# A transformer layer on one NeuronCore: layer-norm sums kept in PSUM, the f32r split handed to ScalarE and GpSimd, and another order of all engines

## The chip, the cores and the metric

One NeuronCore of a Trainium2 chip runs the whole program. The metric is the device time in microseconds (us) of one execution; lower is better. Before the change it is 1008.31 us, the median of three runs (1006.66 to 1008.78).

## What is computed

A batch of 32 sequences of 256 tokens with 128 features passes through one layer: softmax attention with 8 heads (no output projection; each head's values are 128 wide and the heads are summed), a layer norm without scale and shift, a gated feed-forward part with two more hidden layers, and a second layer norm. The reference, cut:

```python
Q = (x @ Wq.T).reshape(b, n, 8, 64)
K = (x @ Wk.T).reshape(b, n, 8, 64)
V = (x @ Wv.T).reshape(b, n, 8, 128)
attn = softmax(einsum('bnhr,bmhr->bhnm', Q, K), axis=-1)
x1 = layernorm(x + einsum('bhnm,bmhd->bnd', attn, V))
h = silu(tlin(x1, w1, s1)) * tlin(x1, w2, s2)      # 128 -> 512
h = gelu(tlin(h, h1, sh1)); h = gelu(tlin(h, h2, sh2))   # 512 -> 512, exact gelu
out = layernorm(x1 + tlin(h, w3, s3))              # tlin(x, w, s) = (x @ w.T) * s
```

Everything is float32.

## The kernel before

**Arithmetic.** TensorE multiplies in float32r. To keep float32 accuracy every operand is split in a high part (a copy rounded to float32r) and a low part (the difference), and a product is three matmuls: high by high, high by low, low by high. The feed-forward weights are ternary, so their low parts are zero; a flag made at run time (`lo_flag`) chooses at a branch on TensorE (line 2009) between a body with and one without these matmuls. The run takes the body without them, and there a feed-forward product is two matmuls.

**Tiles and stages.** The work goes in 16 pairs of sequences (512 tokens, index `i` or `k`). For each pair TensorE makes queries and keys (`query_or_key`, 8 of them, `t` = 0..7), values (`values`, 8), scores (`scores`, 8 groups of 12 matmuls that use 64 rows of the array each and run two at a time), then for each of the 16 head and sequence combinations `u` it turns the normalised probabilities (`turn_prob`, 4 transposes) and multiplies them with the values (`times_v`, 6 matmuls) into PSUM bank 7. The sum over heads is copied to `at` and turned (`turn_attention`), the residual is added (`res_add`), normalised (`stats1_of`, `rstd1_of`, `norm1`) to `x1`, turned again (`turn_x1`), and goes through `layer1_z1`, `layer1_z2`, `layer2`, `layer3`, `layer4` and `turn_y`; `y_add`, `stats2_of`, `rstd2_of` and `norm2` make the output. The last pair's feed-forward part is done in two halves (`..._half`).

**Who does what.** ScalarE (ACT) makes the exponentials, tanh and gelu, and rounds PSUM results to high parts (`t_high`, `v_high`, `pt_high`). VectorE (DVE) makes maxima, reciprocals (`inverse`), low parts of PSUM results (`t_low`, `v_low`, `pt_low`), the gate, and the layer norms. GpSimd (POOL) scales the probabilities in place (`norm`), makes `rstd` by a power, and shares with ACT and DVE the rounding and differences of the hidden activations (`high` and `low`), which lie in SBUF.

**Order.** There is no scheduler at run time. Each engine's order is written out by hand: a start, a loop body `for k in range(1, LAST)` that is unrolled 14 times (on TensorE the function `cycle`), and an end (`last`). In a cycle attention of pair `k`, the queries of pair `k + 1` and the feed-forward part of pair `k - 1` (its third layer's second half and fourth layer: of pair `k - 2`) are interleaved. Engines wait for each other by semaphores; the tuples such as `(s_silu, k - 1, KC, 1)` behind a TensorE step name what it waits for, mostly so that a PSUM bank (the tables `T_BANK` to `YT_BANK`) is free.

**What the steps of the prediction touch.** `norm1` (line 982) reads `res`, mean and rstd from SBUF and writes `x1`; `turn_x1` waits for both halves of it. `res_add` (958) writes its sum to `res` in SBUF, `y_add` (1027) to `y` in SBUF. SyncE (SP) issues all transfers in one queue. The second pair's input is issued last of those at the start:

```python
sp.dma_start(w3_in...); sp.dma_start(res[:, :, :], x_rows[0])...
load_xt(1)      # waits until the single buffer xt_in has been split
```

On ACT `xt_high(1)`, which needs it, stands between `t_high(0, 3)` and `t_high(0, 4)`.

Of the kernel before, what the change touches and what calls it, by code (L numbers as in the profile page):

```python
# [9 lines left out]
ALU = mybir.AluOpType  # L10
# [20 lines left out]
L3_BANK = (2, 5, 0, 6)
L4_BANK = (2,)
YT_BANK = (3,)
# [5 lines left out]
def need(eng, sem, value):  # L39
# [6 lines left out]
T_OTHER = {(0, 0): 1, (0, 1): 5, (0, 2): 2, (0, 4): 3, (0, 5): 1, (0, 6): 1, (0, 7): 5, (1, 0): 4, (1, 1): 5,  # L46
    (1, 2): 4, (1, 4): 2, (1, 5): 3, (1, 7): 5}
V_OTHER = {(0, 0): 2, (0, 2): 3, (0, 3): 1, (0, 5): 1, (0, 6): 0, (0, 7): 2, (1, 0): 0, (1, 1): 2, (1, 2): 0,
    (1, 3): 1, (15, 4): 6, (15, 6): 4, (15, 7): 1}
SC_OTHER = {(0, 0): (5, 6), (0, 1): (3, 0), (0, 2): (1, 6), (0, 3): (4, 0), (0, 4): (3, 2), (0, 5): (5, 3),  # L50
    (0, 6): (1, 6), (0, 7): (5, 1), (1, 0): (6, 4), (1, 1): (5, 3), (1, 2): (4, 6), (15, 3): (2, 6),
    (15, 4): (1, 3), (15, 5): (0, 1), (15, 6): (4, 3), (15, 7): (5, 6)}
TURN_OTHER = {(0, 1): 5, (0, 2): 6, (0, 3): 1, (0, 4): 6, (0, 6): 5, (0, 7): 2, (0, 8): 3, (0, 9): 5, (0, 10): 0,
    (0, 11): 1, (0, 12): 5, (0, 13): 2, (0, 14): 3, (0, 15): 4, (15, 2): 5, (15, 3): 4, (15, 4): 5, (15, 5): 2,
    (15, 6): 3, (15, 7): 4, (15, 8): 6, (15, 9): 2, (15, 11): 1, (15, 12): 4, (15, 13): 5, (15, 14): 2}
AT_OTHER = {(0, 0): 0, (14, 1): 3, (15, 0): 3, (15, 1): 5}
X1T_OTHER = {(14, 0): 4}
Z1_OTHER = {(14, 2): 0, (14, 3): 1}
Z2_OTHER = {(14, 0): 3, (14, 1): 1, (14, 2): 2}
L2_OTHER = {(14, 0): 1, (14, 1): 0, (14, 2): 5, (14, 3): 2}  # L60
L3_OTHER = {(14, 0): 5, (14, 1): 0, (14, 2): 2}
L4_OTHER = {(13, 0): 0, (14, 0): 4}
YT_OTHER = {(13, 0): 0, (14, 0): 5}


X1T_HALF = (5, 3)
Z1_HALF = ((4, 3, 4, 5), (5, 0, 3, 2))
Z2_HALF = ((7, 2, 0, 4), (4, 4, 5, 2))
L2_HALF = ((1, 2, 7, 6), (4, 1, 3, 7))
L3_HALF = ((0, 5, 6, 2), (4, 3, 0, 7))  # L70
L4_HALF = (1, 6)
YT_HALF = (5, 4)


def layer_kernel(nc, x, x_t, wq_t, wk_t, wv_t, w1_t, w2_t, h1_t, h2_t, w3_t, scales_t, out):
# [14 lines left out]
    def there(i):  # L90
        return 0 <= i < PAIRS
# [5 lines left out]
    with ExitStack() as ctx:  # L97
# [38 lines left out]
        with ExitStack() as early:  # L136
# [11 lines left out]
        x1 = sb("x1", [P, TT, D])  # L148
# [101 lines left out]

        def slot(i, u, ring):
            return (i * J + u) % ring
# [13 lines left out]
        def _(sp):  # L266
            sp.dma_start(xt_in[:, :], x_t[0]).then_inc(s_xin, 16)
            sp.dma_start(wq_in[:, A], wq_t[:, A]).then_inc(loads["wqa"], 16)
            sp.dma_start(wk_in[:, A], wk_t[:, A]).then_inc(loads["wka"], 16)
            sp.dma_start(wq_in[:, B_], wq_t[:, B_]).then_inc(loads["wqb"], 16)  # L270
            sp.dma_start(wk_in[:, B_], wk_t[:, B_]).then_inc(loads["wkb"], 16)
            sp.dma_start(wv_in[:, :], wv_t).then_inc(loads["wv"], 16)
            sp.dma_start(scales[:, :], scales_t).then_inc(s_scales, 16)
            sp.dma_start(w1_in[:, :], w1_t).then_inc(loads["w1"], 16)
            sp.dma_start(w2_in[:, :], w2_t).then_inc(loads["w2"], 16)
            sp.dma_start(h1_in[:, :, :], h1_t.rearrange("(c p) o -> p c o", p=P)).then_inc(loads["h1"], 16)
            sp.dma_start(h2_in[:, :, :], h2_t.rearrange("(c p) o -> p c o", p=P)).then_inc(loads["h2"], 16)
# [38 lines left out]
        def _(pool):  # L316
# [1738 lines left out]
```

## Time and profile before

| | |
|---|---|
| median of three runs | 1008.31 us |
| the profiled execution | 1008.28 us |
| its span (first to last instruction) | 1006.5 us |
| mean granted TensorE clock | 0.988 of full |
| busy: PE, DVE, ACT, POOL | 966.8, 882.9, 797.4, 502.2 us |
| length of one cycle, turn_prob(k, 0) to turn_prob(k + 1, 0), k = 2 to 14 | 60.7 us |

PE is TensorE's matmul side and PEld its weight loads, DVE is VectorE, ACT ScalarE, POOL GpSimd and SPq SyncE's queue. L982 is line 982 of the kernel. Times of rows are microseconds from the start of the span unless marked ns. A granted clock of 1.00 is 2.4 GHz, 0.50 is 1.2 GHz.

### The profile page before, as it was taken

To read this page: it belongs to the slowest core of one execution; us is meant where nothing else is said; L and a number is where in the kernel's file an instruction comes from. 1 tells how busy PE (TensorE), PEld (TensorE's weight loads), DVE (VectorE), ACT (ScalarE), POOL (GpSimd) and SP (SyncE) were. 2 spreads that over 40 slices of the span, in tenths; PEclk is the share of its full clock that TensorE was granted. 3 is DMA by queue.
4 is the path that set the end of the run, shared out by engine and by line. 5 is a ranking of instruction groups with operands and counts; after the bars stand their busy time and mean duration, and the time that the engine had idled before them with its cause. 6 is when DMAs were issued, how large, how long until landed. Compare 5 with 4: busy or idle time off the path is not lost.

```text
span 1006.5 us, 19738 instructions
## 1 busy us (share of the span) xinstructions
PE 966.8 (96%) x6553; PEld 821.3 (82%) x6553; DVE 882.9 (88%) x1846; ACT 797.4 (79%) x1958; POOL 502.2 (50%) x520
## 2 busy tenths in 40 slices
PE   4979999999999999999999999999999999999997
PEld 3868888888888888888888888888888888888886
DVE  4988798898988989898898988989898898988886
ACT  3958878888888878878788888878878788888844
POOL 3954354553546345444453545445454553546644
PEclk8989999999999999999999999999999999999999
DMA  5000000000000000010000000000010000000000
GB/s 188 12 13 11 2 21 1 22 11 22 12 2 22 11 22 11 2 32 2 22 12 14 21 1 23 11 22 11 1 33 1 22 12 1 22 1 11 12 11 22
DMA packets 22055, 17.83 MB, mean 18 GB/s; under 512 B 1088, under 2 KB 18496, under 8 KB 21952
## 3 DMA queue, kind: packets, MB, share of 16 engines
q1 hardware_dynamic: 21952, 16.53, 5.6%
q8 instruction: 56, 0.92, 0.4%
q14 instruction: 47, 0.39, 0.1%
HBM read 12.33 MB, written 4.19 MB: 16 GB/s over the span
## 4 chain that ended last, share of the span: by engine, by line
PE 86%; DVE 8%; issue 2%; POOL 1%; DMA 1%; SPq 1%; ACT 1%; POOLq 0%; DVEq 0%; ACTq 0%
PE bank L1567 13%; PE bank L1568 12%; PE bank L1455 12%; PE bank L1449 11%; PE bank L1451 11%; PE bank L1450 10%; PE bank L1498 10%; DVE x L982 5%; PE bank L1547 3%; PE bank L1548 3%; DVE y L1027 1%; DMA xt_in<-in_x_t 1%; DVE res L958 1%; DVE stats L964 1%; PE bank L1627 1%
## 5 line engine op out<-in xcount | busy, mean ns | idle before, releaser
L327 POOL TENSOR_TENSOR prob<-prob,inv_total 128x512 f32<-128x512 f32 x256 | 272.3, 1072 | 179.2 <-DVE inv_total L943 179.2
L538 ACT ACTIVATE prob<-bank,neg_max 128x256 f32<-128x256 f32 x512 | 238.0, 480 | 8.3 <-DVE neg_max L937 7.7
L260 DVE TENSOR_TENSOR pt_lo<-bank,pt_hi 128x512 fp32r<-128x512 f32 x256 | 173.6, 679 | 56.1 <-ACT pt_hi L263 55.9
L263 ACT ACTIVATE pt_hi<-bank 128x512 fp32r<-128x512 f32 x256 | 152.7, 599 | 43.5 <-PE bank L1455 41.4
L937 DVE TENSOR_REDUCE neg_max<-bank 128x2 f32<-128x512 f32 x256 | 171.9, 678 | 5.6 <-PE bank L1498 5.1
L1455 PE MATMUL bank<-ident,prob 128*128 128x128 f32 x1024 | 155.8, 275 | 5.2 <-POOL prob L327 5.2
L1449 PE MATMUL bank<-pt_hi,v_hi 128*128 128x256 f32 x512 | 158.2, 309 | 0.0
L1455 PEld LDWEIGHTS bank<-ident,prob 128*128 128x128 f32 x1024 | 123.3, 142 | 30.1 <-POOL prob L327 5.4
L1451 PE MATMUL bank<-pt_hi,v_lo 128*128 128x256 f32 x512 | 144.9, 283 | 0.0
L1450 PE MATMUL bank<-pt_lo,v_hi 128*128 128x256 f32 x512 | 144.7, 283 | 0.0
L538 ACT ACTIVATION_READ_ACCUMULATOR prob<-bank,neg_max 128x1 f32 x512 | 109.1, 213 | 0.0
L260 POOL TENSOR_TENSOR odd_lo<-gated,odd_hi 128x512 fp32r<-128x512 f32 (+1 forms) x50 | 62.2, 1244 | 83.5 <-ACT odd_hi L263 82.9
L1449 PEld LDWEIGHTS bank<-pt_hi,v_hi 128*128 128x128 f32 x512 | 97.6, 191 | 5.2 <-issue 0.2
L1450 PEld LDWEIGHTS bank<-pt_lo,v_hi 128*128 128x128 f32 x512 | 97.8, 191 | 3.0
L1567 PE MATMUL bank<-even_hi,h_hi 128*128 128x512 f32 x240 | 98.8, 412 | 0.0
L263 ACT ACTIVATE v_hi<-bank 128x512 fp32r<-128x512 f32 x128 | 76.8, 600 | 26.0 <-PE bank L1451 24.8
L1451 PEld LDWEIGHTS bank<-pt_hi,v_lo 128*128 128x128 f32 x512 | 97.3, 190 | 0.0
L1567 PE MATMUL bank<-odd_hi,h_hi 128*128 128x512 f32 x240 | 97.3, 405 | 0.0
L260 DVE TENSOR_TENSOR v_lo<-bank,v_hi 128x512 fp32r<-128x512 f32 x128 | 87.2, 681 | 10.0 <-ACT v_hi L263 10.0
L263 ACT ACTIVATE t_hi<-bank 128x512 fp32r<-128x512 f32 x128 | 76.3, 598 | 23.7 <-PE bank L1451 19.5
L1568 PE MATMUL bank<-odd_lo,h_hi 128*128 128x512 f32 x240 | 94.8, 395 | 0.0
L260 DVE TENSOR_TENSOR t_lo<-bank,t_hi 128x512 fp32r<-128x512 f32 x128 | 86.3, 676 | 9.7 <-ACT t_hi L263 9.4
(137 smaller groups left out, 2395.7 us busy)
## 6 DMA issues: line engine op xcount, KB each, us to landing
xt_in<-in_x_t SPq DMA_DIRECT2D x16, 256.0 KB, 2.7
res<-in_x SPq DMA_DIRECT2D x16, 256.0 KB, 2.8
out_x<-y SPq DMA_DIRECT2D x15, 256.0 KB, 2.6
h_in<-in_h_t SPq DMA_DIRECT2D x2, 1024.0 KB, 9.1
w_in<-in_w_t SPq DMA_DIRECT2D x3, 256.0 KB, 5.7
wv_in<-in_wv_t SPq DMA_DIRECT2D x1, 512.0 KB, 5.1
out_x<-y SPq DMA_DIRECT2D x2, 128.0 KB, 2.0
wq_in<-in_wq_t SPq DMA_DIRECT2D x1, 192.0 KB, 3.5
```

Of the source, the lines that this page charges most:

```text
L260: return eng.tensor_tensor(dst, src, hi.bitcast(F32), ALU.subtract)
L263: return nc.scalar.activation(dst, src, ACT.Copy)
L327: nc.gpsimd.tensor_tensor(prob[:, s, :, :], prob[:, s, :, :], inv_total[:, u, :].unsqueeze(2).to_broadcast([P, NT, N]), ALU.mult).then_inc ...
L538: last = nc.scalar.activation(prob[:, slot(i, u, RING), nt, :], sc_bank(i, u)[:, nt * N:(nt + 1) * N], ACT.Exp, bias=neg_max[:, u, nt:nt + 1],
L937: nc.vector.tensor_reduce(neg_max[:, u, :], sc_bank(i, u).rearrange("p (t m) -> p t m", m=N), AX.X, ALU.max, negate=True).then_inc(s_max, 1)
L1449: mm(dst, w_hi, m_hi, start=start, stop=False)
L1450: mm(dst, w_hi, m_lo, start=False, stop=False)
L1451: return mm(dst, w_lo, m_hi, start=False, stop=stop)
L1455: last = turn(dst[:, n * P:(n + 1) * P], b, ident[:, :])
L1498: ends.append(mm(sc_bank(i, 2 * g + n)[:, nt * N:(nt + 1) * N], left[rows, t, q], right[rows, t + 1, m], start=(term == 0), stop=(term == 2)))
L1567: mm(dst, w_hi[:, c, cols], m_hi[:, c, :], start=begins, stop=False)
L1568: last = mm(dst, w_hi[:, c, cols], m_lo[:, c, :], start=False, stop=ends and not with_lo)
```

## The change

- **Sums in PSUM.** `res_add` and `y_add` write their sums back into the PSUM bank that they read; `stats1_of`, `norm1`, `stats2_of` and `norm2` read them there. `x1` becomes two buffers that alternate. `load_res` now waits for `res_add` and not for `norm1`; `norm2` takes over the wait for the stored `y`.
- **Casts and differences.** All `high` of the hidden activations (12 for each pair) are on ACT and all `low` (12) on POOL; DVE has neither any more outside the last half steps. Before, a cycle's body had 5 `high` on ACT and 7 on DVE, 7 `low` on POOL and 5 on DVE. `xt_high` moves from POOL to ACT and `xt_low` from DVE to POOL. `norm2(13)` and `norm2(14)` move from POOL to DVE. At the start ACT takes the casts of `wqa`, `wqb`, `wkb` and `wv0`.
- **Another order** on all engines, with new bank tables. In a cycle `scores(k, 3)` and `scores(k, 4)` stand together, and `scores(k, 7)` and `scores(k + 1, 0)`; before only `scores(k + 1, 1)` and `(k + 1, 2)` did. `turn_attention(k - 1, 1)` comes third in the cycle, and `turn_x1(k - 1)` some 10 us behind it. The four `gelu3` of a pair are in two groups now, with exponentials between.
- **Start.** `load_xt(1)` stands behind the load of `wv`. Ten matmuls of `ident` by itself (`WARM`) come first on TensorE, into bank 7. Nearly the whole of pair 0's attention stands before the branch.
- `dynamic_dma_scratch_size` goes from 4096 to 2048.

```diff
+WARM = 10
-        x1 = sb("x1", [P, TT, D])
+        x1 = [sb(f"x1_{n}", [P, TT, D]) for n in range(2)]
+        def tiles_in(psum):
+            return psum.rearrange("p (t d) -> p t d", d=D)
+        def sum1_of(i, b):
+            return tiles_in(at_bank(AT_BANK, AT_OTHER, i, b)[:, 0:N])
+        def sum2_of(f):
+            return tiles_in(at_bank(YT_BANK, YT_OTHER, f, 0)[:, :])
...
             sp.dma_start(wv_in[:, :], wv_t).then_inc(loads["wv"], 16)
+            load_xt(1)
             sp.dma_start(scales[:, :], scales_t).then_inc(s_scales, 16)
...
-                    half = res[:, NT * b:NT * (b + 1), :]
-                    nc.vector.tensor_tensor(half, at_bank(...)[:, 0:N].rearrange(...), half,
+                    turned = sum1_of(i, b)
+                    nc.vector.tensor_tensor(turned, turned, res[:, NT * b:NT * (b + 1), :],
                                             ALU.add).then_inc(s_radd, 1)
...
+            def norm(dst, src, tiles, mv, rstd):
+                for t in tiles:
+                    last = nc.vector.tensor_scalar(dst[:, t, :], src[:, t - tiles[0], :], mv[:, t, 0:1], rstd[:, t:t + 1],
+                                                   ALU.subtract, ALU.mult)
+                return last
...
             def norm1(f, b):
                 if there(f):
-                    dve.wait_ge(s_rs1, after(f, 2, b + 1))
-                    need(dve, s_yadd, f)
-                    for t in range(NT * b, NT * (b + 1)):
-                        last = nc.vector.tensor_scalar(x1[:, t, :], res[:, t, :], mv1[:, t, 0:1],
-                                                       rstd1[:, t:t + 1], ALU.subtract, ALU.mult)
-                    last.then_inc(s_x1, 1)
+                    need(dve, s_yadd, f - 1)
+                    hold(dve, s_rs1, after(f, 2, b + 1))
+                    norm(x1_of(f), sum1_of(f, b), tiles_of(b), mv1, rstd1).then_inc(s_x1, 1)
...
+            pe.wait_ge(s_ident, 1)
+            for _ in range(WARM):
+                mm(acc[:, 0:P], ident[:, :], ident[:, :], start=True, stop=True)
             query_or_key(0, 0)
```

The new cycle on TensorE, from its start to `scores(k, 5)` (the branches for k = 1 left out):

```diff
+turn_prob(k, 0, (s_exp, k, J, 4))
+layer3(k - 2, 0, 1, w)
+turn_attention(k - 1, 1, (s_t_lo, k, H, 7))
+layer3(k - 2, 1, 0, w, (s_exp, k, J, 6))
+turn_prob(k, 1, (s_exp, k, J, 5))
+layer3(k - 2, 1, 1, w)
+turn_prob(k, 2, (s_t_lo, k, H, 8))
+scores(k, 3, (s_x1, k - 1, 2, 1), (s_gelu3, k - 2, KC, 1))
+scores(k, 4, (s_gelu3, k - 2, KC, 2), (s_pt_lo, k, J, 1))
+times_v(k, 0)
+layer3(k - 2, 2, 0, w, (s_pt_lo, k, J, 2))
+values(k, 2, (s_x1, k - 1, 2, 2))
+times_v(k, 1)
+layer3(k - 2, 3, 0, w, (s_pt_lo, k, J, 3))
+values(k, 3, (s_exp, k, J, 7))
+values(k, 4, (s_exp, k, J, 8))
+turn_x1(k - 1, (s_v_lo, k, VT, 3))
+turn_prob(k, 3, (s_exp, k, J, 9))
+layer3(k - 2, 2, 1, w)
+layer3(k - 2, 3, 1, w)
+values(k, 5, (s_v_lo, k, VT, 4))
+turn_prob(k, 4, (s_v_lo, k, VT, 5))
+times_v(k, 2)
+turn_prob(k, 5, (s_pt_lo, k, J, 4))
+layer1_z1(k - 1, 0, w, (s_gelu3, k - 2, KC, 3))
+times_v(k, 3)
+layer1_z1(k - 1, 1, w, (s_x1t_lo, k - 1, 1, 1))
+turn_prob(k, 6, (s_pt_lo, k, J, 5))
+times_v(k, 4)
+query_or_key(k + 1, 0, (s_v_lo, k, VT, 6))
+layer1_z2(k - 1, 0, w, (s_pt_lo, k, J, 6))
+scores(k, 5, (s_gelu3, k - 2, KC, 4), (s_silu, k - 1, KC, 1))
```

ACT's order up to the tanh that this last step waits for:

```diff
+pt_high(k, 0)
+gelu3(k - 2, 0)
+pt_high(k, 1)
+gelu3(k - 2, 1)
+pt_high(k, 2)
+high(k - 2, 3, 0)
+high(k - 2, 3, 1)
+exp(k, 6)
...
+x1t_high(k - 1)
+pt_high(k, 3)
+gelu3(k - 2, 2)
+v_high(k, 5)
+pt_high(k, 4)
+high(k - 2, 3, 2)
+gelu3(k - 2, 3)
+pt_high(k, 5)
+tanh(k - 1, 0)
```

## Rows read from the trace of the kernel before

**Rows 1.** The page: engine PE in all, and granted clock in 40 slices.
```profile
PE 966.8 (96%) x6553; PEld 821.3 (82%) x6553; DVE 882.9 (88%) x1846; ACT 797.4 (79%) x1958; POOL 502.2 (50%) x520
...
PEclk8989999999999999999999999999999999999999
```

**Rows 2.** What PE waited for: us in total, times, longest us.
```profile
PE bank L1455 <- DVE x L982: 12.2, 14, 0.9
PE bank L1498 <- DVE t_lo L260: 7.4, 1, 7.4
```

**Rows 3.** Stretches: length, busy PE PEld DVE ACT POOL (instructions), clock, DMA share, GB/s.
```profile
12.90:20.40 7.50, 0.11 (x1) 0.02 (x1) 0.78 (x2) 2.44 (x6) 1.22 (x1) 0.67 0.55 170
20.40:25.63 5.23, 5.22 (x21) 4.17 (x21) 4.67 (x10) 2.65 (x10) 3.17 (x5) 0.50 0.00 0
25.63:64.30 38.67, 38.04 (x305) 32.39 (x303) 36.41 (x78) 34.53 (x108) 30.21 (x31) 1.00 0.03 8
64.30:69.49 5.19, 0.00 (x1) 0.03 (x1) 3.86 (x13) 1.70 (x6) 5.11 (x5) 0.72 0.18 43
69.49:76.80 7.31, 6.78 (x34) 6.14 (x35) 3.23 (x6) 2.91 (x8) 1.19 (x2) 0.50 0.05 14
...
493.94:554.61 60.67, 59.77 (x405) 50.63 (x404) 54.87 (x114) 49.89 (x122) 29.57 (x31) 1.00 0.05 14
```

**Rows 4.** Timeline of cycle 8 about norm1: start, us, engine, line, operation.
```profile
506.22 3.04 POOL L327 TENSOR_TENSOR prob<-prob,inv_total 128x512 f32<-128x512 f32 x3
...
506.35 3.24 DVE L982 TENSOR_SCALAR x<-res,mv,rstd 128x128 f32<-128x128 f32 x4
...
509.65 0.66 PE L1455 MATMUL bank<-ident,x 128*128 128x128 f32 x4 [0.90 <-DVE x L982]
```

**Rows 5.** Chain that ended last, cycle 8: scores alone, and two joined (x24).
```profile
518.63 0.90 PE bank L1498 x12
519.53 0.32 PE bank L1449
519.85 0.12 PE bank L1450
...
543.26 1.62 PE bank L1498 x24
```

**Rows 6.** Timeline of the start: loads, their first users, PE, and cold transposes.
```profile
5.30 0.77 PE L1449 MATMUL bank<-xt_hi,wq_hi 128*128 128x512 f32 x1 [5.30 <-DVE wq_lo L260]
...
8.33 0.61 POOL L346 CAST wv_hi<-wv_in 128x512 fp32r<-128x512 f32 x1 [4.11 <-DMA wv_in<-in_wv_t]
...
9.53 19.01 SPq L284 DMA_DIRECT2D xt_in<-in_x_t  x2
...
17.96 0.63 ACT L263 ACTIVATE xt_hi<-xt_in 128x512 fp32r<-128x512 f32 x1 [7.21 <-DMA xt_in<-in_x_t]
...
69.49 1.94 PE L1455 MATMUL bank<-ident,prob 128*128 128x128 f32 x8 [5.20 <-POOL prob L327]
```

**Rows 7.** Line 2009: duration ns min/median/max, first and last start us.
```profile
L2009 PEldq COMPARE_BRANCH  x1: 4246/4246/4246, 65.1 to 65.1; - x1
```

**Rows 8.** Groups of DVE in cycle 8: busy us, mean ns, idle before.
```profile
L260 DVE TENSOR_TENSOR pt_lo<-bank,pt_hi 128x512 fp32r<-128x512 f32 x16 | 10.9, 680 | 3.5 <-ACT pt_hi L263 3.5
...
L1015 DVE CAST odd_hi<-gelus 128x512 fp32r<-128x512 f32 x5 | 5.0, 1002 | 1.2 <-ACT gelus L592 0.9
...
L260 DVE TENSOR_TENSOR odd_lo<-gelus,odd_hi 128x512 fp32r<-128x512 f32 x2 | 2.2, 1092 | 0.0
...
L1034 DVE TENSOR_SCALAR y<-y,mv,rstd 128x128 f32<-128x128 f32 x4 | 1.1, 338 | 0.0
```

**Rows 9.** Groups of POOL in cycle 8.
```profile
L260 POOL TENSOR_TENSOR odd_lo<-gated,odd_hi 128x512 fp32r<-128x512 f32 x3 | 3.9, 1293 | 5.1 <-ACT odd_hi L263 5.1
```

**Rows 10.** Groups of ACT in cycle 8.
```profile
L538 ACT ACT_TABLE_LOAD x2 | 2.6, 1283 | 0.0
...
L263 ACT ACTIVATE odd_hi<-gated 128x512 fp32r<-128x512 f32 x4 | 2.5, 632 | 0.2 <-DVE gated L1003 0.2
```

More of the change, by code:

```diff
@@ L53 @@
[L53 to L59, printed above, removed]
@@ L737, in _ @@
-                tanh(k - 1, 0)
+                pt_high(k, 3)
[6 more added lines that the diff above has]
+                tanh(k - 1, 0)
+                pt_high(k, 6)
+                high(k - 2, 3, 3)
+                tanh(k - 1, 1)
+                t_high(k + 1, 0)
+                exp(k, 9)
+                exp(k, 10)
+                t_high(k + 1, 1)
@@ L817, in _ @@
+            high(13, 3, 3)
+            high(14, 1, 0)
+            pt_high(15, 6)
+            pt_high(15, 7)
+            tanh(14, 2)
+            v_high(15, 5)
+            high(14, 1, 1)
+            tanh(14, 3)
+            exp(15, 10)
+            yt_copy(13)
+            pt_high(15, 8)
             acc_copy(15, 0)
             high(14, 1, 2)
+            pt_high(15, 9)
+            exp(15, 11)
+            high(14, 1, 3)
+            exp(15, 12)
             exp(15, 13)
-            pt_high(15, 9)
@@ L1206, in _ @@
+            pt_low(0, 14)
+            pt_low(0, 15)
+            flag()
+            inverse(1, 0)
+            inverse(1, 1)
+            res_add(0, 0)
+            stats1_of(0, 0)
+            row_max(1, 4)
+            inverse(1, 2)
+            v_low(1, 0)
+            row_max(1, 5)
+            v_low(1, 1)
+            t_low(1, 6)
+            norm1(0, 0)
             for k in range(1, LAST):
-                v_low(k, 3)
                 inverse(k, 3)
+                t_low(k, 7)
+                res_add(k - 1, 1)
@@ L1341, in _ @@
[L1341 to L1352 removed]
+            silu(14, 0)
+            gate(14, 0)
+            pt_low(15, 4)
+            inverse(15, 8)
+            inverse(15, 9)
+            silu(14, 1)
+            v_low(15, 4)
@@ L1353, in _ @@
+            inverse(15, 12)
+            res_add(15, 0)
+            y_add(13)
             inverse(15, 13)
-            row_max(15, 15)
+            stats1_of(15, 0)
+            pt_low(15, 10)
+            inverse(15, 14)
+            norm1(15, 0)
             stats2_of(13)
-            pt_low(15, 9)
-            high(14, 2, 0)
-            low(14, 2, 0)
-            low(14, 2, 1)
+            pt_low(15, 11)
+            inverse(15, 15)
+            pt_low(15, 12)
+            x1t_low_half(0)
```

1407 lines of the change are left out of this document (663 added, 744 removed).

## Prediction

> **What bounds the kernel now.** I read the page first: PE is busy 96% of the span, and the granted clock dips twice, both times in the first tenth [rows 1]. So the time is PE's own work, plus what PE waits, plus what it does at the low clock. The list of PE's waits names nearly all of the second term: 14 waits for `norm1` (12.2 us), one of 7.4 us in the start [rows 2], and one of 5.2 us at the branch [rows 6]. The stretches then show where the clock is low: PE stands from 12.90 to 20.40, and the 5.2 us of work behind it run at 0.50; it stands from 64.30 to 69.49, and the next 7.3 us run at 0.50 [rows 3]. A cycle is 60.67 us, of which PE is busy 59.77 [rows 3]; the only hole is the 0.90 us before `turn_x1`, whose first transposes are slowed a little too, about 0.97 in all [rows 4]. Without it a cycle is 59.7 us of PE work. DVE, ACT and POOL are busy 54.9, 49.9 and 29.6 us of a cycle [rows 3], so they bound nothing by their sums, only by their order.
>
> **The wait at turn_x1.** `norm1` is four small instructions. Rows 4 show them take 3.24 us, beside three of POOL's `norm` that take 3.04 us; the same operation on `y` has a mean of 338 ns [rows 8]. So `norm1` reading SBUF goes in step with POOL, and PE waits for the fourth. The change takes its input from PSUM and puts `turn_x1` 10 us behind `turn_attention`. I walked the new order with the durations of the rows: the attention turn ends 1.5 us into the cycle, `res_add`, `stats1`, `rstd` and the new place of `norm1` on DVE (behind `row_max(k, 6)`, whose scores end at 5.3) bring `x1` at about 6.5 us; `values(k, 2)`, which now waits for it, stands at 7.8 and `turn_x1` at 11.5. There are 1.3 and 5 us to spare, and even four instructions of 1.03 us more would still be covered at `turn_x1`. **13 cycles x 0.97 = -12.6 us.**
>
> **Joined scores.** One burst of 12 takes 0.90 us and the matmul behind it 0.32 instead of 0.12; two joined take 1.62 [rows 5]. Joining saves 2 x 0.90 - 1.62 + 0.20 = 0.38. A cycle has six bursts instead of seven; other neighbours change by +0.05, so a cycle's PE work goes to 59.4 us. **13 x 0.33 = -4.3 us.** Before the first cycle three joins are lost (+1.1), in the end one is won (-0.4): **+0.7.**
>
> **Casts and differences.** DVE loses seven casts and five differences a cycle, at 0.6 to 1.1 us each [rows 8], `xt_low` and the slow part of `norm1`: some 12 us of 55. POOL gains five differences at 1.29 [rows 9] and `xt_low` for `xt_high`: 30 to 37 us. ACT gains seven casts at 0.63, of which 0.54 count because neighbours overlap, `xt_high` at 0.5, and one more pair of table switches: gelus now come in three groups a cycle, so six loads and not four at 1.28 us, with 0.12 before each [rows 10]. That is 49.9 + 3.8 + 0.5 + 2.8 = 57.0 us busy of 59.4, and this is the change's risk. None of it is on the path as long as no result is late. I walked ACT's order against PE's. It is tight in one place: from `turn_prob(k, 3)` on, ACT does `pt_high`, switch, gelu, `v_high`, `pt_high`, cast, gelu, `pt_high`, switch, tanh; the tanh ends 19.9 us into the cycle and `silu(k - 1, 0)` at 20.6 to 20.7, and `scores(k, 5)`, which needs its bank, is due at 20.6. Elsewhere 0.4 to 2 us are to spare; exponentials and DVE's maxima behind them are the next latest. I take 0.1 us a cycle (0 to 0.9): **+1.3 us.** Behind that waiting PE step every step of the cycle is queued, so it would cost in full.
> The Trainium skill speaks against the third gelu group: its page ScalarE: Activation LUTs, What ACT_TABLE_LOAD costs, gives 2.66 us for every switch, the load and a drain. The trace does not agree: between the instructions on both sides of a load there is hardly more than the 1.283 us itself. By the page the two extra switches would be 5.3 us, ACT would be over its cycle, and rival 2 would be nearer to +2 us a cycle.
>
> **The start.** The load of the second x is issued behind all the weights and ACT, which holds `t_high(0, 4)` and later work behind it, waits 7.21 us [rows 6]. In front of the weights it lands some 1 us behind `wv` (8.3), about when ACT comes to it: PE's 7.5 us [rows 3] go. But `load_xt(1)` waits for `xt_low(0)` (near 4.9), and `scales`, `w1` to `w3` and `res` stand behind it in SP's queue and come about 1 us later. POOL waits for them with `norm(0, 0)` behind; ACT has casts of weights to do between the first `t_high`. By my walk PE then waits 0.7 us for `wkb`, 1.3 us for `turn_prob(0, 0)`, 1.2 us for `turn_prob(0, 1)` and a little at others: I take 3.4 us (1 to 8) in place of 7.5 + 0.6: **-4.7 us.** With no long stand the low clock of 20.40 to 25.63 goes: **-2.6 us** (or 0, if the short waits bring one). PE begins at 5.30 and its first 3.3 us run at the low clock, 1.6 us lost. Ten matmuls of `ident` come before. No row has their form: eight cold transposes take 1.94 us [rows 6], so ten last at least 2.1 us, at most 4.3 us if they are as long as a cold matmul of 512 columns. They run from 1.5, so the queries start between 5.1 and 5.8 us, at the high clock for the most part. I take **-1.5 us** (-1.8 to +0.7).
>
> **The branch.** It takes 4.25 us by itself [rows 7]; PE stands 5.19 us [rows 3] with the load of the flag. The flag comes earlier in the new order, but PE has nothing to do while it branches, wherever the branch stands: **-0.3 us**, a part of the load and the wait for the flag, and the 3.7 us for the low clock behind it stay. The Trainium skill, page Advanced Engine Details and Errata, Control Flow Timing, gives about 108 ns for a compare-and-branch. Here the row shows forty times that, and the measurement decides; by the page the stand would be a wait for data, and the change, which has more work before it, would win 5 us more (979 us).
>
> **The rest.** In cycle 1 the wait for `norm1` goes, -0.3. At the end `norm2(14)` and its store come closer to the last norms: four small instructions on DVE before the last `stats2_half`, **+0.3**. PE's other holes in the last pair (about 3 us) I leave. Bank tables, semaphore names and the scratch size cost nothing.
>
> **Sum.** -12.6 - 4.3 + 0.7 + 1.3 - 4.7 - 2.6 - 1.5 - 0.3 - 0.3 + 0.3 = -24.0 us. Span 1006.5 - 24.0 = 982.5; the execution was 1.8 us longer than its span (1008.28), which is the median of the runs within 0.1. So **984.3 us**.
>
> **Rivals.**
> 1. *Forecast*, 984.3 us, by itself 978 to 990. Chance 0.66.
> 2. *A new wait takes the place of the old.* ACT's chain to `tanh(k - 1, 0)` makes `scores(k, 5)` wait about as long as `turn_x1` did. For: 57 of 59.4 us busy, and no slack there. Against: ACT meets PE's own results several times a cycle, so its lag does not add up. 13 x 0.9 more: 996 us. Chance 0.16.
> 3. *The start keeps its waits.* PE is held by POOL and ACT, which have as much weight work as before, and a second low clock follows: 8 instead of 3.4 us, and the 2.6 us stay: 991.5 us. Chance 0.09.
> 4. *ACT becomes the bound, and it is slower.* ACT stood 10.8 us of each 60.67 us cycle, waiting for PE and others [rows 3]. If it goes on standing as much in its new order, a cycle is 57.0 + 10.8 = 67.8 us. The point from which this decides is a cycle of 61.5 us: (1010.3 - 984.3) / 13 = 2.0 us over the 59.5 of the forecast. At 67.8 us it is 1092 us; a third of the way there is 1020. Against: nearly all its stands are waits for PE, which end sooner when PE is faster. Chance 0.04.
> 5. *It does not do what it says.* `norm1` is as slow from PSUM as from SBUF. DVE's `pt_low` reads PSUM and has a mean of 680 ns with POOL busy half of the time [rows 3, 8], which speaks against. With the distance of 5 us the time stays 984 to 986. Chance 0.05.
>
> **How the numbers follow.** The likeliest is 984. The low end of the range is the forecast with 1 us of waits in the start and none in the cycles, and some of the last pair's holes gone: 977. The high end takes in rivals 2 and 3: 998. A measurement of this kernel can tell 0.2% (2 us) from no change. Faster 0.95: all but rival 4 and 0.01 for what I do not see; the same 0.01; slower 0.04.
>
> **What would show it.** In the profile of after: no wait of PE for `x`; `x` from PSUM at 0.3 us or less each; cycles of 59.4 to 59.6 us; ACT busy near 57 us and POOL near 37 in each; no stand over 2 us before the branch; the branch at 4.2 us again; low clock at the very start and behind the branch only. I am wrong if a cycle shows a wait for `silu`, `exp` or `gelu` of more than 0.3 us, or if PE stands more than 8 us before the branch.

## The result, and the profile after

The changed kernel takes **975.81 us** (median of 4 runs, 975.65 to 976.76); the kernel before, run beside it, 1008.05 us. The ratio is **0.9684, 95% interval 0.9667 to 0.9700**: 32.2 us faster. Forecast were 984.3 us, with a range from 977 to 998: the direction is right, the gain is a third larger than forecast, and the time lies just under the range. The execution profiled here was the longest of the four, 976.76 us with a span of 974.9.

The page of the changed kernel, and what PE waited for in all (us in total, times, longest):

```profile
span 974.9 us, 19735 instructions
PE 960.4 (99%) x6573; PEld 819.3 (84%) x6573; DVE 726.3 (74%) x1653; ACT 881.8 (90%) x2108; POOL 589.4 (60%) x591
...
PEclk9999999999999999999999999999999999999998
```
```profile
PE bank L1452 <- issue: 2.0, 1, 2.0
PE bank L1950 <- POOL ident L335: 1.5, 1, 1.5
PE bank L1495 <- DVE t_lo L277: 0.9, 1, 0.9
PE bank L1452 <- ACT yt L660: 0.6, 1, 0.6
PE bank L1624 <- POOL odd_lo L277: 0.5, 1, 0.5
```

PE is busy 99% of the span, not 96%. Of the slices only the last shows a low clock (8), and it falls there at 969.5 us, behind PE's last matmul; before, two slices in the first tenth were low [rows 1]. Both large waits of before [rows 2] are gone: the 14 for `norm1` (12.2 us) and the one of 7.4 us in the start. DVE has 157 us less to do, ACT 84 and POOL 87 more. The stretches (length, busy PE, PEld, DVE, ACT, POOL, clock) answer to those of before [rows 3]:

```profile
58.76:60.76 2.00, 0.01 (x2) 0.04 (x1) 1.01 (x3) 0.66 (x2) 0.00 (x0) 1.00 0.00 0
60.76:61.58 0.82, 0.82 (x8) 0.82 (x9) 0.00 (x0) 0.16 (x1) 0.00 (x0) 1.00 0.10 20
61.58:64.99 3.41, 3.41 (x25) 3.08 (x25) 2.63 (x9) 1.63 (x3) 1.23 (x3) 0.50 0.26 79
...
469.85:529.15 59.30, 59.30 (x406) 50.48 (x404) 44.47 (x101) 55.64 (x134) 36.09 (x36) 1.00 0.06 15
```

A cycle is 59.30 us, and PE is busy in all of it (before: 60.67, of them 59.77). PE stands 2.0 us at the branch, not 5.2, and the low clock behind it lasts 3.4 us, not over 7. That stretch does not belong to every execution: in the profile of after3 below, the same kernel at 975.43 us, the clock stays high behind the branch:

```profile
60.06:63.47 3.41, 3.41 (x39) 3.11 (x40) 2.52 (x9) 1.68 (x3) 0.41 (x2) 1.00 0.25 67
```

For the sum by terms, both traces were compared step by step. Each matmul has a time from its start to the next one's start, which depends on its kind and its neighbours and is read from cycles without a wait. What a stretch takes beyond these times is its loss. All in us, from the two profiled executions:

| stretch | before | after | measured | forecast |
|---|---|---|---|---|
| the matmuls' own time | 954.9 | 951.3 | -3.6 | -3.6 |
| start: 5.30 or 5.80 to the first query, and losses up to the branch | 17.85 | 9.87 | -8.0 | -8.8 |
| stand at the branch | 5.38 | 2.16 | -3.2 | -0.3 |
| losses behind it, to the end of cycle 1 | 4.37 | 2.74 | -1.6 | -0.3 |
| losses in the 13 full cycles | 12.60 | -1.27 | -13.9 | -11.3 |
| losses in the last pair, and behind the last matmul | 11.36 | 10.12 | -1.2 | +0.3 |
| sum | 1006.5 | 974.9 | -31.5 | -24.0 |

(The -1.27 means that a cycle runs 0.10 us below the table's times.) How much of the cycles' gain stands in the first row and how much in the fifth depends on what is taken as a matmul's own time; together the 13 cycles are 13 x (60.69 - 59.30) = 18.1 us shorter, where 15.6 was forecast. 7.5 of the missing 8.5 us stand in this table; the last 1.0 is that the profiled execution was longer than the median. The experiments went after its rows.

### The profile page after: what moved, and what is told of

Read it like the earlier page. It is cut to its first block, busy times and chain, and to the rows that moved or that the text cites. A ratio compares the mean times of both kernels' runs of the same rounds, so it can differ in the third digit from the quotient of the medians.

```text
span 974.9 us, 19735 instructions
## 1 busy us (share of the span) xinstructions
PE 960.4 (99%) x6573; PEld 819.3 (84%) x6573; DVE 726.3 (74%) x1653; ACT 881.8 (90%) x2108; POOL 589.4 (60%) x591
## 4 chain that ended last, share of the span: by engine, by line
PE 96%; DVE 2%; issue 1%; POOL 1%; ACT 0%; DMA 0%; DVEq 0%; POOLq 0%; ACTq 0%
PE bank L1452 14%; PE bank L1446 13%; PE bank L1564 13%; PE bank L1565 13%; PE bank L1448 12%; PE bank L1447 12%; PE bank L1495 11%; PE bank L1544 3%; PE bank L1545 3%; PE bank L1624 1%; PE bank L1625 1%; PE bank L1950 0%; DVE t_lo L277 0%; DMA out_x<-y 0%; DVE y L1020 0%
## 5 line engine op out<-in xcount | busy, mean ns | idle before, releaser
L342 POOL TENSOR_TENSOR prob<-prob,inv_total 128x512 f32<-128x512 f32 x256 | 262.9, 1043 | 120.9 <-DVE inv_total L989 120.9
L983 DVE TENSOR_REDUCE neg_max<-bank 128x2 f32<-128x512 f32 x256 | 169.8, 679 | 40.5 <-PE bank L1495 40.5
L1446 PE MATMUL bank<-pt_hi,v_hi 128*128 128x256 f32 x512 | 154.4, 302 | 0.0
L277 POOL TENSOR_TENSOR odd_lo<-gelus,odd_hi 128x512 fp32r<-128x512 f32 (+1 forms) x62 | 78.7, 1282 | 63.4 <-ACT odd_hi L280 62.4
L277 POOL TENSOR_TENSOR odd_lo<-gated,odd_hi 128x512 fp32r<-128x512 f32 (+1 forms) x65 | 81.4, 1253 | 53.2 <-ACT odd_hi L280 50.4
L277 POOL TENSOR_TENSOR even_lo<-gelus,even_hi 128x512 fp32r<-128x512 f32 (+1 forms) x66 | 81.7, 1240 | 29.5 <-ACT even_hi L280 29.5
L1565 PE MATMUL bank<-even_lo,h_hi 128*128 128x512 f32 x240 | 94.4, 393 | 0.0
```

Of the source, the lines that this page charges most:

```text
L277: return eng.tensor_tensor(dst, src, hi.bitcast(F32), ALU.subtract)
L342: nc.gpsimd.tensor_tensor(prob[:, s, :, :], prob[:, s, :, :], inv_total[:, u, :].unsqueeze(2).to_broadcast([P, NT, N]), ALU.mult).then_inc ...
L983: nc.vector.tensor_reduce(neg_max[:, u, :], sc_bank(i, u).rearrange("p (t m) -> p t m", m=N), AX.X, ALU.max, negate=True).then_inc(s_max, 1)
L1446: mm(dst, w_hi, m_hi, start=start, stop=False)
L1565: last = mm(dst, w_hi[:, c, cols], m_lo[:, c, :], start=False, stop=ends and not with_lo)
```

## Experiments

The kernel before ran in each group, with a median of 1007.9 to 1008.4 us. The unchanged kernel after, run again as after2 and after3, came out at 975.85 and 976.86 us, ratios 0.9684 and 0.9685. What an edit of after costs is given against these two.

> The kernel after, unchanged, beside the others of this group, to have its time on the same chip: 975.6 to 978 us. The three parts that the sum missed should show again: a stand of 2.0 to 2.2 us at the branch, cycles of 59.30 us, 3.9 to 4.0 us of stands in the last pair.

In after2 the loss at the branch was 2.12 us, a cycle 59.30, the losses of the last pair 3.95: all three as before it.

### What took the wait at turn_x1 away

**n1_sbuf**: the new order, with the sum of `res_add` in SBUF as before. The first of its edits; `stats1_of` and `norm1` read `res` in the same way, and `load_res` waits for `norm1`:

```diff
-                    turned = sum1_of(i, b)
-                    nc.vector.tensor_tensor(turned, turned, res[:, NT * b:NT * (b + 1), :],
-                                            ALU.add).then_inc(s_radd, 1)
+                    half = res[:, NT * b:NT * (b + 1), :]
+                    nc.vector.tensor_tensor(half, sum1_of(i, b), half, ALU.add).then_inc(s_radd, 1)
```

> The kernel after, but res_add writes its sum over res in SBUF and stats1 and norm1 read it there, as before; the new order and the distance of turn_x1 stay. Theory A (the distance took the wait away, PSUM only made the instructions shorter): norm1's instructions go from 0.36 to up to 1.03 us each where POOL's norm runs beside them; the second pair of them ends 1.0 us ahead of values(k, 2) now, which would use that up and at most 0.3 us more a cycle: 976 to 980 us, no wait of TensorE of 0.9 us. Theory B (the sums in PSUM are what took it away): scores(k, 3) or values(k, 2) now wait 0.9 us or more in each of 14 cycles: 988 us or more.

979.46 us, ratio 0.9716 (0.9700 to 0.9732), some 3 us more than after. Line by line (ns min/median/max), `norm1` from SBUF, and then in the kernel after from PSUM:

```profile
L1019 DVE TENSOR_SCALAR x<-res,mv,rstd x64: 334/960/1177, 57.9 to 948.1; 128x128 f32<-128x128 f32 x64
```
```profile
L1020 DVE TENSOR_SCALAR x<-bank,mv,rstd x64: 391/401/411, 58.3 to 946.0; 128x128 f32<-128x128 f32 x64
```

The median is 2.4 times shorter from PSUM, and the spread is gone. PSUM is not faster in itself: the shortest ones from SBUF, which ran with no `norm` of POOL beside them, take 0.33 us. The cycles of n1_sbuf take 59.29 us (two of them 59.49): the wait does not come back there. Cycle 1 has a wait of 2.1 us for `x` at `values(1, 2)`; after3 has one of 0.6 there, so it is 1.5 us more. With 1.3 in the last pair and 0.4 in the full cycles that makes the 3 us. Theory A holds: the new order, in which DVE also has fewer casts and differences, is enough in a full cycle. No run parts the order from DVE's lighter load.

**b_x1later** asked whether distance alone, 0.7 us of it, is enough in the old order.

```diff
-                turn_x1(k - 1, (s_exp, k, J, 10))
                 times_v(k, 2)
+                turn_x1(k - 1, (s_exp, k, J, 10))
```

> The kernel before with turn_x1(k - 1) behind times_v(k, 2), 0.7 us later, and nothing else: norm1 still reads SBUF beside POOL's norm. Theory A (the distance decides): its wait falls from 0.97 to 0.2 us a cycle, 13 x 0.72 = 9.4 us less with its changed neighbours: 998 to 1000 us, norm1 still about 0.8 us an instruction. Theory B (x comes late by whatever is queued on DVE, and the delay shows again at layer1_z1 or query_or_key): 1004 us or more.

1008.35 us, ratio 1.0003 (0.9993 to 1.0013): nothing. The wait at `turn_x1` did fall, from 0.97 to 0.15 us, and 0.41 and 0.34 us came up at the steps behind it. The timeline of cycle 8 shows why:

```profile
506.96 3.25 DVE L982 TENSOR_SCALAR x<-res,mv,rstd 128x128 f32<-128x128 f32 x4
510.13 0.68 DVE L260 TENSOR_TENSOR pt_lo<-bank,pt_hi 128x512 fp32r<-128x512 f32 x1
...
511.33 0.67 DVE L260 TENSOR_TENSOR pt_lo<-bank,pt_hi 128x512 fp32r<-128x512 f32 x1
...
512.15 0.63 PE L1455 MATMUL bank<-ident,prob 128*128 128x128 f32 x4 [0.26 <-DVE pt_lo L260]
```

`norm1` holds DVE for 3.25 us, and the `pt_lo` that PE needs next are queued behind it. The price of a cycle was not the wait for `x`; it was DVE being late by `norm1`, and `x` only the first place where it showed. Theory B, though it named `layer1_z1` or `query_or_key` and the longest wait is now at `turn_prob`. This is so at a distance of 0.7 us more; none of 10 us was tried in the old order.

**b_n1two** took half of DVE's instructions in `norm1` away and left the order alone. It leaves out the second tile's own mean and inverse deviation in each half, and serves only for its time.

```diff
-                    for t in range(NT * b, NT * (b + 1)):
-                        last = nc.vector.tensor_scalar(x1[:, t, :], res[:, t, :], mv1[:, t, 0:1],
-                                                       rstd1[:, t:t + 1], ALU.subtract, ALU.mult)
-                    last.then_inc(s_x1, 1)
+                    t, both = NT * b, slice(NT * b, NT * (b + 1))
+                    nc.vector.tensor_scalar(x1[:, both, :], res[:, both, :], mv1[:, t, 0:1],
+                                            rstd1[:, t:t + 1], ALU.subtract, ALU.mult).then_inc(s_x1, 1)
```

> The kernel before with norm1 as one instruction over both tiles of a half, not one for each: it uses the mean and the inverse deviation of the first tile for both (this leaves out half of the normalisation). It still reads SBUF beside POOL's norm. Two instructions instead of four hold VectorE 1.5 to 2.1 us instead of 3.24. Theory A (the wait of a cycle is VectorE's time in norm1, seen at turn_x1, or at the pt_lo behind it when turn_x1 is moved away): the 0.97 us of each cycle go, cycles of 59.7 to 59.8 us: 995 to 997 us. Theory B (x is late by something ahead of norm1, such as rstd): cycles stay near 60.7 us, 1007 us.

995.07 us, ratio 0.9876 (0.9859 to 0.9892), 12.9 us less. A cycle and the line:

```profile
128.70:188.45 59.75, 59.75 (x405) 50.73 (x404) 53.73 (x112) 49.94 (x122) 29.71 (x31) 1.00 0.05 14
```
```profile
L982 DVE TENSOR_SCALAR x<-res,mv,rstd x32: 405/1062/1128, 81.5 to 964.8; 128x256 f32<-128x256 f32 x32
```

The same line in the kernel before:

```profile
L982 DVE TENSOR_SCALAR x<-res,mv,rstd x64: 333/993/1079, 82.1 to 978.3; 128x128 f32<-128x128 f32 x64
```

Beside POOL's `norm` an instruction over 256 columns takes hardly longer (1.06 us) than one over 128 (0.99): there the number of instructions counts, and the columns hardly. Two fewer of them, and the cycle is 0.94 us shorter; PE waits for nothing in it. Theory A. So either is enough, less DVE time in `norm1` or the new order with its lighter DVE; 0.7 us of distance on PE alone is not.

### The price of a joined burst

**split** parts the joined scores: the second join in all 14 cycles, the first in 13, since cycle 1 keeps it.

```diff
                 if k == 1:
                     scores(k, 4, (s_v_lo, k, VT, 1), (s_pt_lo, k, J, 1))
+                    times_v(k, 0)
                 else:
+                    times_v(k, 0)
                     scores(k, 4, (s_gelu3, k - 2, KC, 2), (s_pt_lo, k, J, 1))
-                times_v(k, 0)
...
-                scores(k + 1, 0, (s_pt_lo, k, J, 11), (s_exp, k, J, 14))
                 layer1_z1(k - 1, 3, w, (s_t_lo, k + 1, H, 4))
+                scores(k + 1, 0, (s_pt_lo, k, J, 11), (s_exp, k, J, 14))
```

> The kernel after with both pairs of joined scores parted in each cycle: times_v(k, 0) stands between scores(k, 3) and scores(k, 4), layer1_z1(k - 1, 3) between scores(k, 7) and scores(k + 1, 0). 27 joins are lost. Theory A (each costs the 0.38 us that the sum took, and nothing hides it since TensorE is the bound in every cycle): 27 x 0.38 = 10.3 us, with the changed neighbours 10.7: 986 to 987.5 us, a cycle 60.1 us. Theory B (the bursts' overhead lies beside other work): 976 to 978 us.

985.85 us, ratio 0.9785 (0.9769 to 0.9801), 9 to 10 us more: theory A's mechanism, just under its range. The cycle, which does not scatter, gives the price: (60.05 - 59.30) / 2 = 0.37 us for a join.

```profile
173.04:233.09 60.05, 60.05 (x405) 50.55 (x404) 44.21 (x101) 55.78 (x134) 35.78 (x36) 1.00 0.05 14
```

PE is busy in all of both cycles: a busy share of 100% hides 0.75 us here that an order of the same matmuls saves.

### The branch

**drain** puts one wait ahead of the flag's load.

```diff
             pe.wait_ge(s_halves, 2)
+            pe.wait_ge(s_t_mm, 2 * H)
             pe.wait_ge(s_flag, 1)
```

> The kernel after with one more wait of TensorE ahead of the load of the flag: that its last matmul before the branch (query_or_key(1, 7)) has ended. Theory A (the sequencer of TensorE runs ahead of its array, and the 2.2 us of matmuls that it has issued cover half of the branch; before, the flag came when the array had run dry): TensorE stands 4.6 to 5.4 us at the branch, not 2.0, and the low clock behind it gets longer: 978.5 to 981.5 us. Theory B (the branch itself has become cheaper, by the code's layout or the smaller scratch): the stand stays under 2.7 us, 975.3 to 976.8 us.

979.89 us, ratio 0.9718 (0.9701 to 0.9734), 3 to 4 us more. The sequencer's two instructions (duration ns, start us) and PE's last matmul before and first behind, in the kernel after:

```profile
L2024 PEldq TENSOR_LOAD <-lo_flag x1: 487/487/487, 56.2 to 56.2; - x1
```
```profile
L2025 PEldq COMPARE_BRANCH  x1: 3813/3813/3813, 56.8 to 56.8; - x1
```
```profile
58.36 0.40 PE L1448 MATMUL bank<-xt_hi,wk_lo 128*128 128x512 f32 x1
60.76 0.41 PE L1452 MATMUL bank<-ident,prob 128*128 128x128 f32 x2 [1.99 <-issue]
```

and the last two with drain:

```profile
58.26 0.40 PE L1448 MATMUL bank<-xt_hi,wk_lo 128*128 128x512 f32 x1
62.88 0.83 PE L1452 MATMUL bank<-ident,prob 128*128 128x128 f32 x4 [4.22 <-issue]
```

In after the load starts at 56.23 and the branch at 56.78, while matmuls go on starting until 58.36: the sequencer is ahead of the array, and about half of load and branch is covered. With drain the load waits until 58.76, the branch is even shorter (3.40 us), and the stand is 4.22 (4.6 to 5.4 was expected). So the code and the scratch are not what made the stand short; theory A. Its other half, a longer low clock behind the longer stand, did not come in the profile: 3.4 us again. In 13 executions of ten kernels in which nothing held the load back, after's among them, exactly 16 matmuls started between the start of the load and the end of the branch; in drain, and in before and its three variants where the flag comes late, none did.

**lead** put larger matmuls among the 16.

```diff
-            values(1, 0, (s_flag, 0, 1, 1))
-            values(1, 1, (s_exp, 1, J, 4))
             times_v(0, 13)
             times_v(0, 14)
             times_v(0, 15)
+            values(1, 0, (s_flag, 0, 1, 1))
+            values(1, 1, (s_exp, 1, J, 4))
```

> The kernel after with times_v(0, 13) to times_v(0, 15) put ahead of values(1, 0) and values(1, 1), so that of the 16 matmuls that TensorE has been issued when the branch begins, 9 are of 512 columns (0.232 us each) and 7 of 256 (0.119 us), not 3 and 13. Theory A (the branch is covered by what is issued ahead, and this is counted in matmuls, not in time): 2.92 us of cover instead of 2.24, so the stand falls from 2.0 to 1.4 us, 0.7 us less. Theory B (issued ahead is a fixed time of some 2.2 us, or the stand has another cause): the stand stays at 2.0 us.

The loss at the branch fell from 2.12 to 1.46 us, just as theory A has it. The time did not fall: 977.05 us, ratio 0.9705 (0.9686 to 0.9724). The first line here is the stand at the branch itself, whose end `v_lo` now sets; the other two, 1.3 us together, are new waits for data behind it:

```profile
PE bank L1452 <- DVE v_lo L277: 1.3, 1, 1.3
PE bank L1452 <- DVE t_lo L277: 0.9, 1, 0.9
PE bank L1452 <- ACT at L280: 0.4, 1, 0.4
```

**b_branch** gives the old kernel the cover: the same steps, the branch 5 us of work later.

```diff
             turn_prob(0, 14, (s_exp, 1, J, 4))
+            turn_prob(0, 15, (s_exp, 1, J, 5))
+            turn_prob(1, 0, (s_pt_lo, 0, J, 14))
+            scores(1, 3, (s_pt_lo, 0, J, 15), (s_t_lo, 1, H, 8))
+            times_v(0, 13)
+            turn_prob(1, 1, (s_flag, 0, 1, 1))
+            times_v(0, 14)
+            times_v(0, 15)
             pe.wait_ge(s_halves, 2)
```

(The same steps are taken out of cycle 1.)

> The kernel before with the branch 5 us of TensorE work later: turn_prob(0, 15), turn_prob(1, 0), scores(1, 3), times_v(0, 13), turn_prob(1, 1), times_v(0, 14) and times_v(0, 15) are put ahead of it; the flag is made when it was. Theory A (5.4 us were lost at the branch since the flag came when TensorE had nothing left; with work issued ahead the branch is half covered): the stand is 1.8 to 2.6 us, and with the shorter stand the low clock behind it is shorter or gone: 3 to 6 us faster than before, 1002.5 to 1005.3 us. Theory B (it is the code behind the branch, or the scratch size of 4096, that makes the branch slow in before): 1008 us within 0.7.

1007.79 us, ratio 1.0000 (0.9990 to 1.0010). It is theory B's number, but not its cause. The loss at the branch did fall, from 5.38 to 2.32 us, but 2.04 us came up at `turn_prob(0, 15)`, whose probabilities were not ready, and another stand of 1.6 us in the first scores behind the branch. Of what PE waited for up to 84 us (the first line is the branch, the second holds the 1.6, the third is `turn_prob(0, 15)`):

```profile
PE bank L1498 <- ACT prob L538: 2.3, 1, 2.3
PE bank L1498 <- issue: 2.0, 2, 1.6
PE bank L1455 <- ACT prob L538: 1.9, 1, 1.9
```

In before, the branch stood on top of waits for data that would have come anyway, and its 5.4 us were worth nothing by themselves. In after a longer stand is paid in full: drain's is 2.2 us longer, and so is its profiled span (977.2 against 974.9 us). A shorter one gains nothing: lead took 0.7 us off, and waits for data came up behind it. Why drain's executions were 3 to 4 us longer in the median, and not 2.2, is open; two of the four had a mean granted clock of 0.994.

### The start

**b_xearly** is `load_xt(1)` behind `wv`, done alone in the old order.

```diff
             sp.dma_start(wv_in[:, :], wv_t).then_inc(loads["wv"], 16)
+            load_xt(1)
...
-            load_xt(1)
             load_xt(2)
```

> The kernel before with the load of the second x behind that of wv, and nothing else: the one edit of the start done alone in the old order. Theory A (the load ended the stand by itself): the 7.47 us wait becomes under 1.5 us, and the 2.6 us of the low clock behind it go: 999 to 1002 us. Theory B (in the old order another wait takes its place: probabilities, weights, or the flag, which is late in any case): 1003 to 1008 us.

999.47 us, ratio 0.9921 (0.9905 to 0.9938), 8.5 us less. Up to the branch PE's waits are:

```profile
PE bank L1455 <- POOL prob L327: 5.8, 1, 5.8
PE bank L1449 <- DVE wq_lo L260: 5.3, 1, 5.3
PE bank L1498 <- DVE t_lo L260: 0.7, 1, 0.7
```

The 7.4 us wait is 0.7, and the low clock behind it is gone. The stand at the branch (listed under `prob`) grew from 5.2 to 5.8, with a branch of 4.83 us. Theory A.

**x_late** is the reverse, in the kernel after.

```diff
             sp.dma_start(wv_in[:, :], wv_t).then_inc(loads["wv"], 16)
-            load_xt(1)
...
+            load_xt(1)
             load_xt(2)
```

> The kernel after with the load of the second x put back behind the loads of all weights. Theory A (this load alone ended the 7.5 us stand in the start): xt_high(1) stands on ScalarE from 11.3 us until the load lands near 18, everything behind it 6 to 7 us later, and a low clock follows the stand: 982 to 986 us. Theory B (the new order of the start would have hidden it, the second pair's first query is at 25.5 us only): 975.8 to 978 us.

981.56 us, ratio 0.9736 (0.9720 to 0.9752), some 5 us more: theory A's mechanism, a low clock behind the stand with it, half a us under its range.

```profile
17.24 0.63 ACT L280 ACTIVATE xt_hi<-xt_in 128x512 fp32r<-128x512 f32 x1 [6.24 <-DMA xt_in<-in_x_t]
...
19.37 0.58 PE L1495 MATMUL bank<-t_hi 64*128 64x256 f32 x2 [5.25 <-DVE t_lo L277]
```

PE needs nothing of the second pair before 25 us; it is held since ACT, in order, has `t_high(0, 5)` behind the waiting `xt_high(1)`.

**no_warm**, **no_warm2** (`WARM = 0`) and **warm8** (`WARM = 8`, not 10), the last two beside **after3**.

> The kernel after without the ten matmuls of ident. The prediction took 1.5 us for them; in the trace of after they last 4.3 us and the queries start at 5.80 us instead of 5.30, but at the high clock from 6.9 on. Theory A (they gain what the lower clock would cost, less 0.5 us of delay, and some of it is lost in the waits for weights behind): 975.8 to 977 us. Theory B (the full 1.5 us): 977.3 us. Theory C (they cost more than they give): 975.3 us or less.

> The kernel after without the ten matmuls of ident, again. Theory A (they pay 3 to 4 us, since without them most executions have a second stretch at the low clock in or behind the start): 978.5 to 980.5 us and a clock of 0.994 to 0.995 in most executions. Theory B (the 3.7 us of the first look were chance, the profile's 0 to 1 us is right): 976 to 977.3 us.

> The kernel after with eight matmuls of ident instead of ten. They end near 4.9 us, ahead of the first query's data (5.15 us), where ten end at 5.80. Theory A (the first query is held by the warming matmuls): 0.3 to 0.6 us less than after. Theory B (the short idle time ahead of the first query, or the fewer matmuls, let the clock stay low longer): the same or up to 3 us more.

> The kernel after, unchanged, beside the next two: 975.5 to 976.5 us, with a mean granted clock of 0.997 to 0.999 in most executions.

no_warm gave 979.58 us (ratio 0.9717), no_warm2 978.85 (0.9709, 0.9696 to 0.9722), after3 976.86 (0.9685, 0.9672 to 0.9699), **warm8 975.40 (0.9674, 0.9661 to 0.9687)**. The ten matmuls are worth 2 to 3.7 us, more than the 1.5 of the sum and more than any theory of no_warm had it; in the second group the two intervals just touch. The first rows of PE, of no_warm2, after3 and warm8:

```profile
5.30 0.77 PE L1446 MATMUL bank<-xt_hi,wq_hi 128*128 128x512 f32 x1 [5.30 <-POOL wq_lo L277]
```
```profile
1.51 4.33 PE L1950 MATMUL bank<-ident 128*128 128x128 f32 x20 [1.51 <-POOL ident L335]
5.60 0.48 PE L1446 MATMUL bank<-xt_hi,wq_hi 128*128 128x512 f32 x1
```
```profile
1.51 3.78 PE L1950 MATMUL bank<-ident 128*128 128x128 f32 x16 [1.51 <-POOL ident L335]
```

Cold, ten matmuls of `ident` last 4.1 to 4.3 us (each is two records), the upper bound of the forecast. The profiled executions differ by 1.0 us (no_warm, after) and 1.8 (no_warm2, after3); the rest goes with the mean granted clock of the executions: 0.994 to 0.996 in seven of the nine without them, 0.997 to 0.999 in nine of the thirteen of after, and 0.998 in all five of warm8. What makes the clock fall in one execution and not in another is not settled. warm8 has the lowest median of all the kernels that ran; against after its gain lies within the intervals. Its first query does start at 5.30, but the matmuls follow each other every 0.43 us until 7.15, not every 0.23, and its profiled span is after3's, 973.6 us: theory A's gain does not show there.

### How tight ScalarE is

**act4** and **act8** put small copies ahead of the place that the prediction held to be tight.

```diff
+        spare = sb("spare", [P, 10, 32])
...
+                for n in range(10):
+                    copy(spare[:, n, :], h1_hi[:, 0, 0:32].bitcast(F32))
                 tanh(k - 1, 0)
```

> The kernel after with ten more small copies of 128x32 on ScalarE ahead of tanh(k - 1, 0) in every cycle, some 1.7 to 2.5 us, into a tile that nobody reads. The prediction held ScalarE's chain to be tight there (0 to 0.1 us). In the trace of after, silu(k - 1, 0) ends 1.35 us ahead of scores(k, 5), and ScalarE stands 3.6 us of a cycle. Theory A (1.35 us is the slack of the tightest place): scores(k, 5) waits 0.3 to 1.2 us in each of 14 cycles, and not more elsewhere: 980 to 993 us. Theory B (other results of ScalarE are later still, or its lag adds up): over 1000 us. Theory C (the slack is larger than it looks, since ScalarE's own waits for TensorE take the copies in): 977.5 us or less.

> The kernel after with twenty small copies (128x16) on ScalarE ahead of tanh(k - 1, 0), 2.4 us by the 0.12 us apiece of the run with ten, of which 1.20 us passed without a wait of TensorE. Theory A (the slack of ScalarE's chain to silu(k - 1, 0) is 1.35 us, and there its lag ends): scores(k, 5) waits 1.0 to 1.1 us in each of 14 cycles, 990 to 992 us. Theory B (other results are held up too): 993 us or more. Theory C (ScalarE's stands take it in): 978 us or less.

The first: 976.11 us, ratio 0.9681 (0.9665 to 0.9697), as after. This is theory C's time, but not for its reason: the ten copies take 1.20 us (1.7 to 2.5 was expected), less than the slack. In the kernel after, `silu(k - 1, 0)` starts at 488.41 and `scores(k, 5)` at 490.43:

```profile
488.41 0.67 DVE L1050 SCALAR_TENSOR_TENSOR gated<-tanh_out,bank 128x512 f32<-128x512 f32 x1
...
490.43 0.39 PE L1495 MATMUL bank<-t_hi 64*128 64x256 f32 x2
```

With twenty (`range(20)`, 128x16), it is 988.37 us, ratio 0.9805 (0.9790 to 0.9820), 11.5 to 12.5 us more: a cycle of 60.23 us, of which ACT is busy 57.28, and one wait in each:

```profile
PE bank L1498 <- DVE gated L1053: 9.7, 14, 0.7
```

So 0.93 us a cycle where 1.05 was expected: theory A's wait, 1.6 us under its range in time. The chain has 1.35 us of slack (490.43 less the end of `silu` at 489.08), its lag does not add up, and no other wait comes up in the cycles.

## Why the prediction was nearly right, and where it failed

- **The wait at turn_x1**, 12.6 us: the size is right, and all of it went. Its cause is half right. The forecast put it down to the slow `norm1` and the distance to `turn_x1`; b_x1later shows that 0.7 us of distance alone gives nothing, b_n1two that DVE's time does. That even slow instructions would be covered in the new order was right (n1_sbuf, 0.4 us in all full cycles); whether the order or DVE's lighter load covers them is not shown. The rival "it does not do what it says" is refuted: 0.40 us from PSUM, 0.96 from SBUF.
- **Joined scores**, 4.3 us: right; 0.37 us for a join by split, 0.38 forecast. With the neighbours it came to 0.42 a cycle (0.32 by the table, and the 0.10 below it) where 0.33 stood: 1.2 us more.
- **The new wait at scores(k, 5)**, +1.3 us: did not come. The failed step is the walk of ACT's order: it had the tanh end 19.9 us into the cycle, and its `silu` starts at 488.41 - 469.85 = 18.6. ACT is busy 55.6 us of a cycle, where 57.0 were summed. act8 shows the mechanism to be real, and to begin some 1.4 us later. This and the joins are the 2.6 us of the cycles.
- **The start**, -8.8 us forecast and -8.0 measured: the load is worth 8.5 us in the old order and 5 in the new. It had been forecast at 4.7 + 2.6 = 7.3. The warming matmuls save 2 to 3.7 us over many executions, not 1.5, though they hold the first query to 5.60 or 5.80. One term was too large and one too small, so that their sum came out within 0.8 us is in part luck.
- **The branch**, -0.3 us forecast and -3.2 measured: the largest miss. The failed step is the sentence that PE has nothing to do while it branches, wherever the branch stands. It was read from a row where the flag came late and the array had run dry; drain and the count of 16 show that with the flag in time about half of load and branch is covered: 2.16 us are lost, where drain loses 4.39 and before 5.38. The price of about 108 ns from the Trainium skill (Advanced Engine Details and Errata, Control Flow Timing) was rightly set aside: no run here has a branch under 3.39 us. But with it I set aside that a later branch could win anything, and it did win, by its cover and not by its price.
- **Behind the branch**, -0.3 forecast, -1.6 measured: the low clock is 3.4 us long in the profiled execution, not over 7. The shorter stand is not shown to be the reason: it is 3.4 us in drain too, with a stand of 4.22. It is there in the profiles of after, after2, drain and no_warm, and in none of the other nine of after and its variants; where it is missing (after3), PE waits 0.6 us for `x` in cycle 1 instead.
- **The end**, +0.3 forecast, -1.2 measured: "about 3 us of holes that I leave" were 5.85, and are 3.95 in the new order. The longest, for `odd_lo` before the second layer of the first half, went from 1.14 to 0.53 us; behind the last matmul it is 0.7 us more. No run separates the parts of this; that the new order of the last pair does it is only argued.

What the prediction wanted to see in the profile, against what stands there: no wait for `x` in a cycle (none in this execution, 0.6 us in cycle 1 of after3); `x` from PSUM at 0.3 us or less (0.40); cycles of 59.4 to 59.6 us (59.30); ACT near 57 and POOL near 37 us busy (55.6 and 36.1); no stand over 2 us ahead of the branch but the one at the very start (0.9 at most); the branch at 4.2 us (3.8).

The misses nearly all have one sign: where the trace did not show an effect of the new order, the likeliest value was taken as "stays". The low end of the range, 977, was made of 2.4 us in the start, 1.3 in the cycles and the 3 of the last pair; it had nothing for the branch, the low clock behind it or a larger gain from the joins.

## What to carry to other kernels

A wait names the result that came last, not the cost: before moving the consumer, look at how long the producer's engine is held and what else is queued on it. A stand that covers another wait is worth nothing until that one is gone too, so price it with the engines behind it and not from its length. Put a branch where its flag has long been made and the sequencer has work issued ahead.

## What the runs showed of the hardware

- TensorE's sequencer was 16 matmuls ahead of the array at the branch in each of the ten kernels where no wait held it: 2.24 us of cover with 3 matmuls of 512 columns and 13 of 256, 2.9 with 9 and 7. The branch itself took 3.39 to 4.83 us.
- VectorE's `tensor_scalar` of 128x128 took 0.40 us from PSUM beside GpSimd's 128x512 `tensor_tensor`. From SBUF it took 0.33 with nothing of GpSimd beside it, and up to 1.18 beside that instruction (medians over all: 0.96 in n1_sbuf, 0.99 in before); at 128x256 the median was 1.06. GpSimd's own operation stayed at 1.04.
- Ten matmuls of 128x128 f32 at the very start took 4.1 to 4.3 us and show as 20 records. Two profiled executions with the same span (after3 and warm8, 973.6 us) began with ten and with eight.
- Entering and leaving a burst of scores costs 0.37 us that no busy share shows: PE is busy in all of a cycle with and without the joins.
- Copies of 128x32 on ScalarE follow each other every 0.12 us, though each is shown with 0.25.
